# Scores by 32-row products, and a new order on TensorE and GpSimd, in an attention and mixture-of-experts kernel

## What is computed

```
n  = layernorm(x)
q, k, v = n @ Wq + bq, ctx @ Wk + bk, ctx @ Wv + bv      # 16 heads of 16 channels
p  = softmax(q k^T / 4, within blocks of 64 tokens)       # other blocks are masked out
x1 = x + (p v) @ Wo + bo
y  = layernorm(x1)
w  = top-2 of softmax(y @ gate_w^T + expert_bias), normalised
m  = sum over the two chosen experts of w_e * (gelu(y @ up_e^T) @ down_e^T)
out = x1 + layernorm(m) + y
```

## Time and profile before

| | us |
|---|---|
| median of 3 runs | 828.54 |
| lowest, highest | 825.12, 830.93 |
| the profiled execution | 830.71 |
| its span | 828.9 |
| mean granted TensorE clock in it | 0.94 of 2.4 GHz |

### The profile page before, as it was taken

The page is one execution under the profiler, slowest core; times in us unless marked ns, Lnnn a source line. Parts: engine busy times, 40 slices in busy tenths (PEclk is TensorE's granted clock), DMA queues, the critical chain, the costliest instruction groups (busy, mean ns, idle before and its releaser), DMA issues. The chain is left out here.

```text
span 828.9 us, 20886 instructions
## 1 busy us (share of the span) xinstructions
PE 720.5 (87%) x6385; PEld 643.8 (78%) x6386; DVE 558.2 (67%) x1399; ACT 387.1 (47%) x729; POOL 356.3 (43%) x487
## 2 busy tenths in 40 slices
PE   5999999999999971699999999999999999999000
PEld 4899888888888861599989999999998999998000
DVE  5778988989898868565566655555556665553494
ACT  3877877777786553122333333333333333332143
POOL 2765688778887647011222222211122222222396
PEclk9999999999999985699999999999999999999555
DMA  4443333333331312211111111111111111100693
GB/s 170 149 156 104 96 105 122 125 114 110 122 129 47 113 69 91 66 40 53 53 51 51 51 51 51 44 39 45 51 51 51 51 51 51 51 24 22 223 302 104
DMA packets 41525, 71.58 MB, mean 86 GB/s; under 512 B 5440, under 2 KB 26432, under 8 KB 41472
## 3 DMA queue, kind: packets, MB, share of 16 engines
q1 hardware_dynamic: 33648, 50.47, 19.5%
q0 software_dynamic: 6816, 18.88, 5.9%
q10 hardware_dynamic: 1008, 1.55, 0.5%
HBM read 47.81 MB, written 25.23 MB: 88 GB/s over the span
## 5 line engine op out<-in xcount | busy, mean ns | idle before, releaser
L1200 POOL DMA_INDIRECT y_rows<-area x78 | 75.8, 972 | 344.2 <-ACT area L1078 331.5
L608 PE MATMUL ps_a<-area,w_hi 128*128 128x256 f16 x1248 | 207.7, 274 | 1.7 <-DVE area L911 1.7
L622 PE MATMUL ps_b<-w_hi,area 128*128 x1248 | 206.4, 273 | 0.0
L608 PE MATMUL ps_a<-area,w_lo 128*128 128x256 f16 x624 | 170.7, 274 | 0.0
L622 PE MATMUL ps_b<-w_lo,area 128*128 x624 | 170.1, 273 | 0.0
L1071 ACT ACTIVATE area<-ps_a 128x512 f32<-128x512 f32 x156 | 93.2, 597 | 116.0 <-PE ps_a L608 114.5
L608 PEld LDWEIGHTS ps_a<-area,w_hi 128*128 x1248 | 122.4, 98 | 16.1 <-issue 2.1
L622 PEld LDWEIGHTS ps_b<-w_hi,area 128*128 128x128 f16 x1248 | 122.1, 98 | 14.1
L909 DVE TENSOR_SCALAR area<-ps_c 128x512 f16<-128x512 f32 x39 | 27.0, 691 | 142.4 <-PE ps_c L592 142.4
L1078 ACT ACTIVATE area<-ps_b,slot_w 128x256 f32<-128x256 f32 x78 | 32.7, 470 | 185.1 <-PE ps_b L622 185.1
L928 DVE SCALAR_TENSOR_TENSOR area<-area 128x512 f16<-128x512 f32 x156 | 109.2, 700 | 5.4
(11 more groups left out here) (149 smaller groups left out, 1233.8 us busy)
## 6 DMA issues: line engine op xcount, KB each, us to landing
area<-weights SPq DMA_DIRECT2D x32, 512.0 KB
area<-xs_rows SPq DMA_DIRECT2D x39, 264.0 KB, 2.6
w_hi<-y_rows SPq DMA_DIRECT2D x32, 256.0 KB, 4.5
pay<-x_in SPq DMA_DIRECT2D x32, 128.0 KB, 3.7
area<-ctx_t SPq DMA_DIRECT2D x32, 128.0 KB
out<-w_lo SPq DMA_DIRECT2D x16, 256.0 KB, 2.4
xs_rows<-route_consts SPq DMA_DIRECT2D x8, 264.0 KB, 4.6
y_rows<-area POOLq DMA_INDIRECT x78
```

The lines of the kernel that those rows point to most:

```text
L608: mm = pe.matmul(ps_h[:, q, (ic % 2) * SLOTS:(ic % 2 + 1) * SLOTS], w[:, bass.ds(first + (hc * I + ic * P), P)], r[b][:, hc, :], start=(n ...
L622: mm = pe.matmul(ps_y[:, b, v * D:(v + 1) * D], g[b][:, ic, v * P:(v + 1) * P], w[:, bass.ds(first + (EXPERT_COLS + ic * D), D)], start=(n ...
L1200: pool.indirect_dma_start(y_rows[:, :], bass.IndirectOffsetOnAxis(ap=didx[b][:, v:v + 1], axis=0), y_s[b][:, v * D:(v + 1) * D], None).the ...
```

## The change

It has five parts.

1. The output bias product takes all 128 rows (the others are zero) instead of two.
2. The keys are no longer doubled and masked. One VectorE instruction adds the biases to queries and keys at once (`qk_b`). The scores are 16 products of 32 rows and 64 columns (32 passes) in four strips of the array, which write to the lower halves of the four banks of `ps_a`. Values, gate rows, output product, logits and ranks move to upper halves of the same banks. So the scores now wait for what is read from there: the sum of tile i-3, the logits of tile i-4, the values of tile i-1, the gate's rows of tile i-4, and a group's ranks; and the value product and the gate's transposes wait for the scores to be read (`sub_r`).
3. On TensorE the scores come after the transposes of the probabilities.
4. A group's ranks are read from PSUM by `take_ranks`, two steps after `group_seen` right after L665 and so ahead of L671 and the logits; `positions` uses the copy. Several waits for x1, logits and positions go, and ScalarE's L1034 no longer waits for the value product.
5. On GpSimd `w_lo` comes ahead of `q_m`.

```
-        ps_s = ps_a[:, 0:2, :].rearrange("p a (s x k) -> p (a s) x k", s=2, k=BLOCK)
+        ps_s = ps_a[:, :, 0:D].rearrange("p s (x k) -> p s x k", k=BLOCK)
...
-        ps_v = ps_a[:, 2, 0:D]
-        ps_x2t = ps_a[:, 2, D:2 * D].rearrange("p (c n) -> p c n", c=HC)
-        ps_wo, ps_lg = ps_a[:, 3, 0:D], ps_a[:, 3, D:D + E]
+        ps_v = ps_a[:, 0, D:2 * D]
+        ps_x2t = ps_a[:, 1, D:2 * D].rearrange("p (c n) -> p c n", c=HC)
+        ps_wo, ps_lg = ps_a[:, 2, D:2 * D], ps_a[:, 3, D:D + E]
...
 TensorE, a step (the transposes of the probabilities now stand before this)
-                    pe.wait_ge(k_r, HC * (t + 1))
+                    pe.wait_ge(qb_r, t + 1)
                     since(pe, sub_r, t)
+                    since(pe, v_r, 2 * t)
+                    since(pe, x2t_r, t - 3)
+                    since(pe, x1_r, t - 2)
+                    since(pe, lg_r, t - 3)
+                    for g in range(NG):
+                        if in_body(g) and t == group_seen(g) + 2:
+                            pe.wait_ge(rank_r, g + 1)
                     for c in range(HC):
                         for n in range(NB):
-                            for a in range(HALVES):
-                                r = slice(a * P // HALVES, (a + 1) * P // HALVES)
-                                mm = pe.matmul(ps_s[:, 2 * a:2 * a + 2, c * NB + n, :],
-                                               q_m[r, c, n].rearrange("p h q -> p (h q)"),
-                                               k_bd[r, c, :, n, :], start=True, stop=True)
+                            for a in range(STRIPS):
+                                r = slice(a * P // STRIPS, (a + 1) * P // STRIPS)
+                                mm = pe.matmul(ps_s[:, a, c * NB + n, :], q_m[r, c, n].rearrange("p h q -> p (h q)"),
+                                               k_b[r, c, n, :], start=True, stop=True)
...
-                        since(pe, v_r, 2 * (min(t + 3, TILES) if isinstance(t, int) else t + 3))
+                        pe.wait_ge(sub_r, min(t + 4, TILES))
...
                     pe.wait_ge(ctx_lo_r, t + 1)
+                    pe.wait_ge(sub_r, t + 1)
...
-                    pe.matmul(to, sel16[0:2, :], bo_rows[0:2, :], start=True, stop=False)
+                    pe.matmul(to, sel16, bo_rows, start=True, stop=False)
...
 VectorE
-                    if not last_out(t):
-                        since(dve, lg_ps, t)
                     r = pay[:, t, 0:D]
-                    dve.tensor_tensor(r, ps_wo_last if last_out(t) else ps_wo, r, ALU.add).then_inc(x1_r, 1)
+                    dve.tensor_tensor(r, ps_wo, r, ALU.add).then_inc(x1_r, 1)
+                for g in range(NG):
+                    if in_body(g) and 2 * j + u == group_seen(g) + 2:
+                        take_ranks(g)
...
-                    dve.tensor_tensor(q_b, ps_q, bq_s.unsqueeze(2).to_broadcast([P, HC, P]), ALU.add).then_inc(qb_r, 1)
-                    for c in range(HC):
-                        dve.scalar_tensor_tensor(k_bd[:, c].rearrange("p s b k -> p s (b k)"), ps_k[:, c, :].unsqueeze(1).to_broadcast([P, 2, P]),
-                                                 bk_s[:, c:c + 1],
-                                                 cst[:, C_SMASK:C_SMASK + 2].unsqueeze(2).to_broadcast([P, 2, P]),
-                                                 ALU.add, ALU.mult).then_inc(k_r, 1)
+                    dve.tensor_tensor(qk_b, ps_qk, bqk_s.unsqueeze(2).to_broadcast([P, 2 * HC, P]), ALU.add).then_inc(qb_r, 1)
...
+            def take_ranks(g):
+                size = GROUP_SIZES[g]
+                dve.wait_ge(rank_ps, g + 1)
+                if in_body(g):
+                    dve.wait_ge(lg_ps, min(group_seen(g) - 1, TILES))
+                dve.tensor_tensor(of(g, pos_f), ps_rank(g).rearrange("p (e t) -> p e t", e=E), per_e(g, ebase_e), ALU.add).then_inc(rank_r, 1)
...
 GpSimd, after ctx_lo
+                t = chunk_at(i)
+                if t is not None and t < WSTEPS - LATE:
+                    cols = slice(t * WCOLS, (t + 1) * WCOLS)
+                    pool.wait_ge(w_hi_r, t + 1)
+                    pool.tensor_tensor(w_lo[:, cols], staging[t % 2], w_hi[:, cols], ALU.subtract).then_inc(w_lo_r, 1)
                 t, half, b = here(j, u, 1)
...
                                        ALU.mult).then_inc(q_r, 1)
-                t = chunk_at(i)
-                if t is not None and t < WSTEPS - LATE:
-                    cols = slice(t * WCOLS, (t + 1) * WCOLS)
-                    pool.wait_ge(w_hi_r, t + 1)
-                    pool.tensor_tensor(w_lo[:, cols], staging[t % 2], w_hi[:, cols], ALU.subtract).then_inc(w_lo_r, 1)
```

More of the change, by code:

```diff
@@ L30 @@
 STRIPS = 4
-HALVES = 2
 NB = P // BLOCK
@@ L123, in program @@
         ident = cst[:, C_ID:C_ID + P]
-        bq_s, bk_s, bv_s = (cst[:, n:n + 2] for n in (C_BQ, C_BK, C_BV))
+        bqk_s, bv_s = cst[:, C_BQ:C_BQ + 2 * HC], cst[:, C_BV:C_BV + 2]
         gate_w = cst[:, C_GATE:C_GATE_B].rearrange("p (c e) -> p c e", c=HC)
@@ L257, in program @@
         table_r, code_r, resid_r = sem("table_r"), sem("code_r"), sem("resid_r")
-        seen_r = sem("seen_r")
+        seen_r, rank_r = sem("seen_r"), sem("rank_r")
         xt_ps, xt_r = sem("xt_ps"), sem("xt_r")
@@ L261, in program @@
             sem(n) for n in ("wv_scaled", "wv_hi_r", "wv_lo_r", "ctx_scaled", "ctx_hi_r", "ctx_lo_r"))
-        q_r, qb_r, k_ps, k_r, v_ps, v_r = (sem(n) for n in ("q_r", "qb_r", "k_ps", "k_r", "v_ps", "v_r"))
+        q_r, qb_r, k_ps, v_ps, v_r = (sem(n) for n in ("q_r", "qb_r", "k_ps", "v_ps", "v_r"))
         s_ps, max_r, sub_r, p_r, pt_ps, pt_r = (sem(n) for n in ("s_ps", "max_r", "sub_r", "p_r", "pt_ps", "pt_r"))
@@ L444, in step @@
                     mm.then_inc(xt_ps, 1)
-                t, half, b = here(j, u, 0)
-                if valid(t):
-                    pe.wait_ge(q_r, t + 1)
-                    pe.wait_ge(k_r, HC * (t + 1))
-                    since(pe, sub_r, t)
-                    for c in range(HC):
-                        for n in range(NB):
-                            for a in range(HALVES):
-                                r = slice(a * P // HALVES, (a + 1) * P // HALVES)
-                                mm = pe.matmul(ps_s[:, 2 * a:2 * a + 2, c * NB + n, :],
-                                               q_m[r, c, n].rearrange("p h q -> p (h q)"),
-                                               k_bd[r, c, :, n, :], start=True, stop=True)
-                    mm.then_inc(s_ps, 1)
                 t, half, b = here(j, u, -1)
@@ L466, in step @@
                     mm.then_inc(pt_ps, 1)
+                t, half, b = here(j, u, 0)
+                if valid(t):
+                    pe.wait_ge(q_r, t + 1)
+                    pe.wait_ge(qb_r, t + 1)
+                    since(pe, sub_r, t)
+                    since(pe, v_r, 2 * t)
[5 more added lines that the diff above has]
+                            pe.wait_ge(rank_r, g + 1)
+                    for c in range(HC):
+                        for n in range(NB):
+                            for a in range(STRIPS):
+                                r = slice(a * P // STRIPS, (a + 1) * P // STRIPS)
+                                mm = pe.matmul(ps_s[:, a, c * NB + n, :], q_m[r, c, n].rearrange("p h q -> p (h q)"),
+                                               k_b[r, c, n, :], start=True, stop=True)
+                    mm.then_inc(s_ps, 1)
                 t, half, b = here(j, u, 1)
@@ L473, in step @@
                     since(pe, qb_r, t)
-                    since(pe, k_r, HC * t)
                     for c in range(HC):
@@ L526, in step @@
                     pe.wait_ge(ot_r, 2 * (t + 1))
[L527 to L534, removed]
+                    since(pe, x1_r, t)
                     if t == 0:
                         pe.wait_ge(bo_made, 5)
-                    to = ps_wo_last if last_out(t) else ps_wo
-                    pe.matmul(to, sel16[0:2, :], bo_rows[0:2, :], start=True, stop=False)
+                    to = ps_wo
+                    pe.matmul(to, sel16, bo_rows, start=True, stop=False)
                     for h in range(2):
@@ L547, in step @@
                             pe.wait_ge(fixed_r, 5)
-                        if not valid(here(j, u, -2)[0]):
-                            pe.wait_ge(x1_r, TILES)
-                        pe.wait_ge(lg_r, min(here(j, u, -3)[0], TILES))
+                        since(pe, lg_r, here(j, u, -3)[0])
                         rank(g)
@@ L559, in step @@
                         if in_body(g) and 2 * j + u == group_seen(g) + 2:
-                            pe.wait_ge(pos_r, g + 1)
+                            pe.wait_ge(rank_r, g + 1)
                     for k in range(HC):
@@ L705, in step @@
                 if 2 * j + u == group_seen(NG - 2) + 1:
+                    take_ranks(NG - 2)
                     positions(NG - 2)
@@ L827, in shares @@
```

(9 more changed lines are left out.)

29 lines of the change are left out of this document (12 added, 17 removed).

## The result

The changed kernel takes 853.96 us (median of 4 runs, 851.35 to 855.85) against 829.35 (825.12 to 830.93) for the one before, measured together: a ratio of 1.0303, 95% interval 1.0255 to 1.0351. It is slower by 24.6 us where 13 were forecast, and lies outside the range. The profiled execution took 854.12 us, its span 851.9.

What follows compares the result with a forecast made beforehand. Attention was taken as bound by TensorE, VectorE 14% behind. Five cycles +10, four steps before +1.8, last four +0.8: +12.6, called +13; 843.5 against the profiled 830.7, 841.5 against the 828.5 median. Range 817 to 850.

Steps and rivals of the forecast that it cites:

- The bias product: TensorE's output bias product over all 128 rows avoids two array shape changes: -0.2 us per step, bounds 0 and -0.3.
- The scores' passes: TensorE's scores as 32 half-width passes in four strips still take 1.10 us, a difference of zero, up to +1.1 per step.
- rival C: TensorE's scores cost by number of passes, 2.20 us, making the unstalled step 9.52 and the time 852; chance 0.08.
- The unstalled step: An attention step on TensorE without waits for VectorE takes 8.42 us, against 8.62 before.
- w_lo in an ordinary step: GpSimd's w_lo runs from 3.15 to 5.28 us after the scores' start T, catching VectorE's normalisation.
- Biased queries and keys: On VectorE one 512-column instruction takes 0.6 us in place of three taking 1.13, saving 0.5 per step.
- The group's step 11.0: The attention step completing a routing group: next scores wait for VectorE's logits and start 10.97 us after its own scores.
- One long scores' wait per group: Listed sign of a right forecast: once per routing group TensorE's scores wait long for VectorE's read of the logits (L676).
- The step 9.1: An ordinary attention step, its row transposes waiting for the caught normalisation, takes 9.07 us instead of 8.62.
- Rival A: w_lo starts after the normalisation, so no collision: ordinary steps 8.42, cycle 34.9, about -8 us, 820; chance 0.30.
- the term of the five cycles and of the last four steps: Attention's five four-step cycles at 38.2 instead of 36.2 us, +10; its last four steps 37.5 instead of 36.7, +0.8.
- The start: The attention stage up to the scores of tile 3: forecast difference 0.

Runs made afterwards that it cites:

- 6: Kernel before, with only the output bias product taking all 128 rows instead of two; 825.19 us, ratio 0.9973 to the kernel before.
- 13: Changed kernel with GpSimd's w_lo cut from 1024 to 32 columns, experts reading w_hi for the rest; 821.08 us, ratio 0.9928 to the kernel before.
- Experiment 7: Changed kernel plus 11 unused TensorE products ahead of the scores' wait in the step after a group; 843.21 us, ratio 1.0201 to the kernel before.
- 3: Changed kernel with the second choice one step later and ScalarE's choice exponentials behind the probabilities' copy; 837.31 us, ratio 1.0131 to the kernel before.
- 14: Kernel before with GpSimd's w_lo cut from 1024 to 32 columns, experts reading w_hi for the rest; 819.16 us, ratio 0.9907 to the kernel before.
- 1: Changed kernel with GpSimd's w_lo put back behind the masked queries q_m; 854.43 us, ratio 1.033 to the kernel before.
- 2: Changed kernel with w_lo, still ahead of q_m, waiting until VectorE's gate-row normalisation is done; 852.31 us, ratio 1.0317 to the kernel before.
- 15: Changed kernel with w_lo back behind q_m, second choice one step later, shares ahead of the biased queries; 830.72 us, ratio 1.0045 to the kernel before.
- 12: Kernel before with the bias product over 128 rows and the second choice one step later; 820.11 us, ratio 0.9914 to the kernel before.
- 16: Kernel before with 128-row bias product, second choice one step later and shares ahead of the biased queries; 821.78 us, ratio 0.9948 to the kernel before.
- 11: Changed kernel with w_lo back behind q_m and the second choice one step later; 844.41 us, ratio 1.02 to the kernel before.
- 5: Kernel before with only GpSimd's order changed, w_lo ahead of q_m; 860.40 us, ratio 1.0416 to the kernel before.

## Why the prediction was wrong

**Right.** The bias product: -0.2 forecast, 0.30 measured (6). The scores' passes: 1.05 us, so rival C is out. The unstalled step: 8.42 forecast, 8.33 measured. w_lo in an ordinary step at T + 3.15: T + 3.11. L707's median 1.7: 1731 ns. L511 waiting for it: 9.4 us in 18 steps. The second choice's first instruction (L794, before L803) at 0.19. Biased queries and keys 0.6: 0.68. The group's step 11.0: 10.8 to 11.1. One long scores' wait per group for the logits: 1.3 us. The step 9.1: 8.93 to 9.45. The stretch from tile 31 on, 0: -0.9 us. Rival A needed w_lo's start after T + 3.68. That came in one step only, tile 10, with w_lo at T + 3.80, L707 at 0.41 us and a step of 8.33. Where the collision was taken away in all steps (13), the cycle was 34.6 against rival A's 34.9.

**Wrong: the term of the five cycles and of the last four steps.** The sum took the step behind a group as one more step of 9.07, at a clock of 1.00. It was 11.6 in three of six groups and 10.1 in one, since TensorE's new wait at the end of the group's step let the clock fall to 1.2 GHz. I had named this and put it into the range's upper end only, without a price, though the wait stood in my own working: a group's step of 10.97, where TensorE alone needs 9.07, leaves 1.9 us of it (1.3 measured). Experiment 7 sizes the term: with TensorE at work in that wait, the cycles grow by 11.8 for a forecast of 10 and the last four steps by 0.8 for 0.8. The missing term is 4.9 us in the cycles and 3.1 in the last four steps, 8.0 in all. The spans of the two profiles differ by 23.0 us for a sum of 12.6, so the clock is 8.0 of the 10.4 us that were missing. Experiments 3 and 13 agree: there the scores wait 0.5 and 1.1 us at most in the cycles, and the clock stays at 1.00.

**Smaller misses.** The start: +1.8 us at tile 3, where I had 0. It is there in experiment 13 too (38.23), so it is not w_lo. It lies in the step of tile 0, 8.80 us against 6.98 before. There the value product meets one of its new waits, the one for the scores to be read (L696):

```profile
19.75 1.44 PE L524 MATMUL ps_a<-area 128*128 128x256 f16 x6 [0.92 <-DVE area L696]
```

The granted clock is 0.50 from 18 to 21 us, and the probability transposes at 21.72 still take 1.73 us instead of 1.04, while before the value product at 20.17 already ran at its full 0.82. How the 1.8 us divide between the wait and the clock was not tested.

The steps that end a cycle are 9.45 instead of 9.07. There GpSimd is late behind its sends, w_lo starts at T + 3.62, just ahead of the normalisation, and holds it for its whole length:

```profile
184.10 2.13 POOL L1139 TENSOR_TENSOR w_lo<-area,w_hi 128x1024 f16<-128x1024 f32 x1
184.13 2.25 DVE L707 TENSOR_SCALAR pay<-pay,area 128x256 f32<-128x256 f32 x1
```

In the working, "843.5 against it" should be 843.3 (830.7 and 12.6); the forecast does not rest on it.

**What the loss is made of.** Without the low weights' work the two kernels differ by 1.9 us (13, 14; their intervals overlap), of which 1.4 stand at tile 3 already; with it by 24.6. So the loss is the meeting of that work with VectorE and what follows from it. Its place alone does not explain it (1, 2), nor do the new waits alone, which are all still there in 13. In the old layout a blocked VectorE instruction in the routing delays only VectorE; in the new one the scores' banks hold the logits, and any lateness of VectorE at the end of a step reaches TensorE and then its clock. Moving w_lo only changes which instruction is caught: normalisation, first choice, second choice, shares. Putting w_lo back and moving the caught instructions recovers most of the loss (15: the ratio falls from 1.0303 to 1.0045, 21 us), and leaves the new layout 0.5% behind the old kernel, not ahead of it. On the old layout the late second choice and the bias product give 0.9914 (12), and with the shares moved too 0.9948 (16): with like moves the old layout stays ahead.

Not settled: what share of the start's 1.8 us is the clock, whether the new order on TensorE, which no run moves alone, gains anything, and why the same idle time lets the clock fall behind some groups and not behind others.

## What to carry to other kernels

Before two engines' buffers are put into one PSUM bank, list what the leading engine will then wait for, and read from the trace of before how late that is in the worst step of the cycle, not in an ordinary one. An instruction moved on GpSimd must be placed in every kind of step against the VectorE instructions that it can hold, as here the normalisation, the choices and the shares; if no place is free, move the small VectorE work, and look at what then waits for GpSimd (15, 16). And when a forecast puts a new idle time of a microsecond into an engine that ran at full clock, give the clock a term of its own in the sum.

## What the runs showed of the hardware

TensorE's granted clock fell from 1.00 to 0.50 after one idle time of 1.32 us inside a stage in which it was otherwise busy, and stayed there for 6.8 us (tile 20 of the kernel after). It did so behind four of six groups there, behind all six with the same 1.31 to 1.33 us in experiment 2, and behind all six with 3.0 to 3.3 us in experiment 1. It fell behind two of four waits of 0.91 to 0.96 us in experiment 16, and behind none of seven of 1.06 to 1.30 us in experiment 13. So the length of one idle time does not settle it. Half-precision products whose result is thrown away kept it at 1.00 (experiment 7).

A 2.13 us GpSimd instruction held VectorE instructions of 0.17 to 0.40 us for as long as it still ran: 2.15 us on 32 columns (experiment 1), 1.88 on 4 (11), 2.26 on 256 (5). An addition with one input in PSUM (L657 under w_lo in experiment 11, 0.42 us) and a reduction (L816 there, 0.21 us) were not held.

32 float32 passes of 32 rows and 64 columns in four strips take 1.05 us, as long as 16 of 64 rows and 128 columns in two.
